# Pair attention layer on one core: front stage in two-part fp32r, separate semaphores for its loads, right values read back chunk by chunk, a seventh place for them in the mixing stage

## The reference

```
lk, rk, lv, rv = (x @ W_lk), (x @ W_rk), (x @ W_lv), (x @ W_rv)      # x: (2, 64, 64, 256), 8 heads of 32
scores = einsum('bxahd,bayhd->bxayh', lk, rk) / sqrt(32)
att    = softmax(scores, axis=2)                                      # over a
o      = einsum('bxayh,bxahd,bayhd->bxyhd', att, lv, rv)
...
```

## Time and profile before

| | |
|---|---|
| median of 3 runs | 3948.43 us (3945.7 to 3954.97) |
| the profiled execution: its own time | 3949.96 us |
| the profiled execution: span | 3947.9 us |
| PE busy | 3542.7 us (90%) |
| DVE busy | 2868.5 us (73%) |
| ACT busy | 2432.3 us (62%) |
| POOL busy | 1322.5 us (33%) |
| instructions fetched by DMA (q8) | 170 packets, 2.79 MB |
| DMA, 275 to 295 us, while batch 1's exponents are stored | 416 GB/s |

### The profile page before, as it was taken

How to read it: one execution, slowest core, us unless ns; L and a number is a source line. 1 busy time by engine, 2 the same in 40 slices (tenths; PEclk the granted TensorE clock), 3 DMA queues, 4 the chain that set the end, 5 groups by cost and what they waited for, 6 DMA issues and landing times. The chain is left out here.

```text
span 3947.9 us, 81665 instructions
## 1 busy us (share of the span) xinstructions
PE 3542.7 (90%) x30559; PEld 2953.9 (75%) x30559; DVE 2868.5 (73%) x4303; ACT 2432.3 (62%) x6245; POOL 1322.5 (33%) x740
## 2 busy tenths in 40 slices
PE   8986888788869988999999979999999979788887
PEld 5644555455549986888888868888888878788886
DVE  1457999899968874677777755777777766677787
ACT  3545888788855554666656655666666632677776
POOL 0007999899955552000000001000000014222254
PEclk9988999999989998999999989999999989899999
DMA  4583111311123333000000011000000046555565
GB/s 125 172 230 78 43 41 40 80 43 43 43 61 105 118 99 112 1 17 17 17 19 25 12 53 65 17 17 17 17 17 12 12 138 213 162 137 136 139 217 169
DMA packets 204756, 303.82 MB, mean 77 GB/s; under 512 B 18464, under 2 KB 156576, under 8 KB 201376
## 3 DMA queue, kind: packets, MB, share of 16 engines
q1 hardware_dynamic: 195232, 291.51, 24.7%
q10 hardware_dynamic: 9216, 8.39, 0.6%
HBM read 199.18 MB, written 100.66 MB: 76 GB/s over the span
## 5 line engine op out<-in xcount | busy, mean ns | idle before, releaser
L661 POOL TENSOR_TENSOR mx_big<-mp_lvs,mx_big 128x1280 f32<-128x1280 f32 (+1 forms) x256 | 802.0, 3205 | 335.0 <-ACT mp_lvs L587 317.1
L640 DVE TENSOR_TENSOR mx_big<-mp_psL,mx_big 128x2816 f32<-128x2816 f32 (+1 forms) x256 | 786.6, 3147 | 39.1 <-PE mp_psO L532 32.1
L594 ACT ACTIVATE mp_cut<-mp_psO,mx_mask 128x128 f32<-128x128 f32 x2048 | 551.0, 404 | 145.1 <-PE mp_psO L532 114.6
L532 PE MATMUL mp_psO<-mx_big,mp_pair 128*16 128x256 f32 x8192 | 501.5, 385 | 107.6 <-DVE mx_big L640 75.0
L1298 PE MATMUL sv_psO<-at_v_hi,sv_p_hi 128*128 128x258 f32 x2048 | 583.2, 285 | 13.2 <-DVE sv_p_lo L1386 10.1
L1298 PE MATMUL sv_psO<-at_v_lo,sv_p_hi 128*128 128x258 f32 x2048 | 578.1, 282 | 0.0
L1298 PE MATMUL sv_psO<-at_v_hi,sv_p_lo 128*128 128x258 f32 x2048 | 577.9, 282 | 0.0
L1317 ACT COPY sv_S<-sv_psS 128x512 f32<-128x512 f32 x512 | 300.5, 587 | 378.4 <-PE sv_psS L1272 260.7
L532 PEld LDWEIGHTS mp_psO<-mx_big,mp_pair 128*16 128x16 f32 x8192 | 330.1, 126 | 242.5 <-DVE mx_big L640 135.9
L1361 DVE TENSOR_TENSOR sv_run<-sv_run,sv_S 128x512 f32<-128x512 f32 x448 | 314.5, 702 | 248.1 <-ACT sv_S L1317 247.0
L1386 DVE TENSOR_TENSOR sv_p_lo<-sv_S,sv_p_hi 128x512 fp32r<-128x512 f32 x512 | 353.8, 691 | 108.4 <-ACT sv_p_hi L1326 107.4
(11 more groups left out here) (244 smaller groups left out, 7446.7 us busy)
## 6 DMA issues: line engine op xcount, KB each, us to landing
re_xg<-xg SPq DMA_DIRECT2D x192, 384.0 KB, 3.3
xg<-ga_xg SPq DMA_DIRECT2D x32, 768.0 KB, 4.0
att<-mx_big SPq DMA_DIRECT2D x16, 1024.0 KB, 5.5
mx_big<-rv SPq DMA_DIRECT2D x16, 1024.0 KB, 17.4
mp_pair<-att SPq DMA_DIRECT2D x128, 128.0 KB, 2.9
fr_xr<-in_x SPq DMA_DIRECT2D x16, 512.0 KB, 4.7
fr_xl<-in_x SPq DMA_DIRECT2D x32, 256.0 KB, 4.3
rv<-fr_rvs SPq DMA_DIRECT2D x16, 512.0 KB, 3.0
```

The lines of the kernel that those rows point to most:

```text
L532: mm = pe.matmul(psO[32 * j:32 * j + 2 * H, c % 2, q, :], pair[:, s, :, :, c * YC + y], Z[:, c % 2, y, :], start=True, stop=True, tile_pos ...
L594: ins = nc.scalar.activation(cut[:, s, c, :, h * DK:(h + 1) * DK], psO[:, c % 2, :, h * DK:(h + 1) * DK], ACT.Copy, scale=mask[:, h:h + 1])
L640: nc.vector.tensor_tensor(Z[:, c % 2, 0:m], psL[:, s, 0:D].unsqueeze(1).broadcast_to([P, m, D]), big[:, rv_slot(b, c), 0:m], ALU.mult).the ...
L661: nc.gpsimd.tensor_tensor(Z[:, c % 2, m:YC], lvs[:, s, :].unsqueeze(1).broadcast_to([P, YC - m, D]), big[:, rv_slot(b, c), m:YC], ALU.mult ...
```

## The change

- **fp32r parts.** The weights and the turned tiles of the front stage are kept as two fp32r parts, hi (a rounded copy, ACT) and lo (the value less hi, DVE), and each product is three fp32r matmuls (hi·hi, lo·hi, hi·lo) where it was one fp32 matmul. The original weights lie in `rvs`. PSUM `psT` is given free by DVE, after lo.
- **Order of a block.** PE: rk products, score of the block before, xl turned, rv products, xr of the *next* block turned, lk products. ACT: keep, xl hi, up to two exponents, two rvs copies, xr hi of the next block, the remaining exponents, two lk copies. DVE: two rk copies (now after the score of the block before), xl lo, the maximum, half of the block's subtractions and sums, xr lo of the next block, the other half.
- **Loads.** Own semaphores for ident and each weight; the xr tile of block 0 before the weights, xl after them; the three constants of the mixing stage last.
- **rv back.** Chunk 0 of batch 0 is read after block 14, chunk 1 when chunk 0 has landed, chunk 2 among the last stores, chunk 3 in the mixing stage behind pair 0's loads.
- **Late sums.** `PE_SUMS = (0, 8)`: all of batch 1's sum is on PE, 64 matmuls of 256 columns; DVE inverts straight from PSUM.
- **Mixing.** Seven places for rv (`seventh` is a buffer of its own). Chunks 0 to 2 of batch 1 are each loaded after two pairs' loads in the first pairs; chunk 3 at the change of batch, behind pair 33's x. Loads of x no longer wait for the memsets, which have the `pair` tiles ahead of `psO`. The loops of DVE and POOL start at pair 2.

```diff
+RV_SLOTS = 7
+Z_SLOT = 6
+def rv_place(big, seventh, b, c):
+
+    n = (b * (N // YC) + c) % RV_SLOTS
+    return seventh if n == RV_SLOTS - 1 else big[:, n]
...
-    PE_SUMS = (0, 5)
-    SUBS = {8: range(0, 6), 9: range(6, 13), 10: range(13, NHALF)}
-    EXPS = {9: range(0, 4), 10: range(4, 8), 11: range(8, 12), 12: range(12, NHALF)}
-    SUMS = {11: range(1, 8), 12: range(8, 12), 13: range(12, NHALF)}
+    PE_SUMS = (0, NC)
+    SUBS = {8: range(0, 4), 9: range(4, 9), 10: range(9, 14), 11: range(14, NHALF)}
+    EXPS = {9: range(0, 4), 10: range(4, 9), 11: range(9, 14), 12: range(14, NHALF)}
+    SUMS = {11: range(1, 4), 12: range(4, 9), 13: range(9, 14), 14: range(14, NHALF)}
...
+        w_hi = {n: fr.sb(f"w{n}_hi", [P, KT, D], F32R) for n in W}
+        w_lo = {n: fr.sb(f"w{n}_lo", [P, KT, D], F32R) for n in W}
+        xrT_hi, xrT_lo, xlT_hi, xlT_lo = (fr.sb(n, [P, KT, BLK], F32R) for n in ("xrT_hi", "xrT_lo", "xlT_hi", "xlT_lo"))
+        w = {n: rvs[:, i // 2, i % 2 * KT:(i % 2 + 1) * KT, :] for i, n in enumerate(W)}
...
-                sp.dma_start(*loads[0]).then_inc(w_in, 16)
-                load(0)
-                for dst, src in loads[1:]:
-                    sp.dma_start(dst, src).then_inc(w_in, 16)
-                load(1)
+                sp.dma_start(ident[:, :], ident_d).then_inc(ident_in, 16)
+                load_xr(0)
+                for n, src in (("rk", w_rk), ("rv", w_rv), ("lk", w_lk)):
+                    sp.dma_start(w[n][:, :, :], k_rows(src)).then_inc(w_in[n], 16)
+                load_xl(0)
+                load_xr(1)
+                load_xl(1)
+                for dst, src in mix_loads:
+                    sp.dma_start(dst, src).then_inc(mix_in, 16)
                 for j in range(NJ):
                     if j + 2 < NJ:
-                        load(j + 2)
+                        load_xr(j + 2)
+                        load_xl(j + 2)
...
-                        for c in range(N // YC):
-                            load_rv(sp, big, rv_d, 0, c, rv_back)
+                        load_rv(sp, big[:, 0], rv_d, 0, 0, rv_back)
+                sp.wait_ge(rv_back, 32)
+                load_rv(sp, big[:, 1], rv_d, 0, 1, rv_back)
                 for k in range(NC):
                     save(1, k)
-                sp.wait_ge(rv_back, 32 * (N // YC))
+                    if k == NC // 2 - 1:
+                        load_rv(sp, big[:, 2], rv_d, 0, 2, rv_back)
+                sp.wait_ge(mix_in, 16 * len(mix_loads))
+                sp.wait_ge(rv_back, 96)
...
+                def terms(hi, lo, xT_hi, xT_lo):
+
+                    return [(a, c, k) for k in range(KT) for a, c in ((hi, xT_hi), (lo, xT_hi), (hi, xT_lo))]
+
+                def units(g, n, xT_hi, xT_lo, done):
+                    for e, (a, c, k) in enumerate(terms(w_hi[n], w_lo[n], xT_hi, xT_lo)):
+                        mm = pe.matmul(psP[:, g, :], a[:, k, g * P:(g + 1) * P], c[:, k, :], start=(e == 0), stop=(e == 3 * KT - 1))
                     mm.then_inc(done, 1)
...
-                pe.wait_ge(w_in, 16 * len(loads))
+                def turn_xr(j):
+                    pe.wait_ge(xr_in[j % 2], (j // 2 + 1) * 16)
+                    reach(pe, xlT_kept, j)
+                    turn(xr, j % 2, xr_turned)
+
+                pe.wait_ge(ident_in, 16)
+                turn_xr(0)
                 for j in range(NJ):
-                    s = j % 2
-                    pe.wait_ge(xr_in[s], (j // 2 + 1) * 16)
-                    reach(pe, xlT_kept, j)
-                    turn(xr, s, xr_turned)
+                    pe.wait_ge(xrT_kept, j + 1)
+                    pe.wait_ge(w_cut, 1)
+                    for g in range(G):
+                        reach(pe, lk_kept, (j - 1) * G + g + 1)
+                        units(g, "rk", xrT_hi, xrT_lo, rk_made)
                     if j > 0:
                         score(j - 1)
-                    pe.wait_ge(xl_in[s], (j // 2 + 1) * 32)
-                    pe.wait_ge(xrT_kept, j + 1)
-                    turn(xl, s, xl_turned)
-                    for g in range(G):
-                        reach(pe, lk_kept, (j - 1) * G + g + 1)
-                        units(g, wrk, xrT, rk_made)
+                    pe.wait_ge(xl_in[j % 2], (j // 2 + 1) * 32)
+                    turn(xl, j % 2, xl_turned)
+                    pe.wait_ge(w_cut, 2)
                     for g in range(2):
                         pe.wait_ge(rk_kept, j * G + g + 1)
                         for t in range(2):
-                            for k in range(KT):
-                                mm = pe.matmul(psP[:, g, t * D:(t + 1) * D], xrT[:, k, (2 * g + t) * P:(2 * g + t + 1) * P], wrv[:, k, :],
-                                               start=(k == 0), stop=(k == KT - 1))
+                            rows = slice((2 * g + t) * P, (2 * g + t + 1) * P)
+                            for e, (a, c, k) in enumerate(terms(w_hi["rv"], w_lo["rv"], xrT_hi, xrT_lo)):
+                                mm = pe.matmul(psP[:, g, t * D:(t + 1) * D], c[:, k, rows], a[:, k, :], start=(e == 0), stop=(e == 3 * KT - 1))
                         mm.then_inc(rv_made, 1)
+                    if j + 1 < NJ:
+                        turn_xr(j + 1)
+                    pe.wait_ge(xlT_kept, j + 1)
+                    pe.wait_ge(w_cut, 3)
                     for g in range(G):
-                        if g == 0:
-                            pe.wait_ge(xlT_kept, j + 1)
                         pe.wait_ge(rv_kept, j * 2 + g + 1)
-                        units(g, wlk, xlT, lk_made)
+                        units(g, "lk", xlT_hi, xlT_lo, lk_made)
...
-                    for u in range(AB // 2):
-                        mm = pe.matmul(psS[:, 0, :], ident[:, :], E[1][:, r + 2 * u:r + 2 * u + 2, :].rearrange("p a f -> p (a f)"),
-                                       start=(k == 0 and u == 0), stop=(k == PE_SUMS[1] - 1 and u == AB // 2 - 1))
+                    for u in range(AB):
+                        mm = pe.matmul(psS[:, 0, 0:F], ident[:, :], E[1][:, r + u, :],
+                                       start=(k == 0 and u == 0), stop=(k == PE_SUMS[1] - 1 and u == AB - 1))
...
+                keep_xrT(0)
+                for n in ("rk", "rv", "lk"):
+                    act.wait_ge(w_in[n], 16)
+                    nc.scalar.copy(w_hi[n][:, :, :], w[n][:, :, :]).then_inc(w_hi_cut, 1)
                 for j in range(NJ):
-                    act.wait_ge(xr_turned, j + 1)
-                    nc.scalar.copy(xrT[:, :, :], psT[:, :, :]).then_inc(xrT_kept, 1)
+                    exps = list(EXPS.get(j, ()))
                     if j > 0:
                         keep(j - 1)
                     act.wait_ge(xl_turned, j + 1)
-                    nc.scalar.copy(xlT[:, :, :], psT[:, :, :]).then_inc(xlT_kept, 1)
-                    exps = list(EXPS.get(j, ()))
-                    for k in exps[:3]:
+                    nc.scalar.copy(xlT_hi[:, :, :], psT[:, :, :]).then_inc(xlT_hi_kept, 1)
+                    for k in exps[:2]:
...
+                    if j + 1 < NJ:
+                        keep_xrT(j + 1)
+                    for g in range(G):
                         if g == 0:
-                            for k in exps[3:]:
+                            for k in exps[2:]:
                                 exponent(0, k)
-                    for g in range(G):
...
                         dve.wait_ge(pe_summed, 1)
-                        for u in range(2):
-                            fold(den[:, b, 1 + u, :], last, psS[:, 0, u * F:(u + 1) * F])
-                            last = den[:, b, 1 + u, :]
+                        last = psS[:, 0, 0:F]
+                    else:
+                        dve.wait_ge(dve_summed, sums[0])
+                        fold(sum4[:, 0:2, :], sum4[:, 0:2, :], sum4[:, 2:4, :])
+                        fold(sum4[:, 0, :], sum4[:, 0, :], sum4[:, 1, :])
+                        last = sum4[:, 0, :]
...
+                keep_lo(0, xrT_hi, xrT_hi_kept, xrT_lo, xrT_kept)
+                for i, n in enumerate(("rk", "rv", "lk")):
+                    dve.wait_ge(w_hi_cut, i + 1)
+                    nc.vector.tensor_tensor(w_lo[n][:, :, :], w[n][:, :, :], w_hi[n][:, :, :], ALU.subtract).then_inc(w_cut, 1)
                 for j in range(NJ):
                     for g in range(G):
                         dve.wait_ge(rk_made, j * G + g + 1)
+                        if j > 0:
+                            dve.wait_ge(scored, j)
                         nc.vector.tensor_copy(rk[:, g, :], psP[:, g, :]).then_inc(rk_kept, 1)
-                        if j > 0:
-                            most(j - 1, g)
+                    keep_lo(j, xlT_hi, xlT_hi_kept, xlT_lo, xlT_kept)
+                    if j > 0:
+                        for u in range(2):
+                            most(j - 1, u)
                     if j == NC:
                         most_of_all(0)
-                    for k in SUBS.get(j, ()):
```

(51 more changed lines are left out.)

71 lines of the change are left out of this document (36 added, 35 removed).

## The result

The changed kernel takes **3913.12 us** (median of 4 runs, 3905.99 to 3916.29), the kernel before 3951.07 (4 runs): a ratio of 0.9902, 95% interval 0.9883 to 0.9922. The forecast was 3915, in a range of 3897 to 3936. The profiled execution is the fastest of its four, 3905.99 us with a span of 3904.2; the span fell by 43.7 us where the sum gave 34.8. So the median came within 2 us of the forecast, while the sum, which was made for the profiled execution, is 9 us off there.

The account below looks back on a forecast made before the run. PE was taken to bound the front stage, DVE to be nearly always busy in mixing. Front-stage blocks -38.4, gaps +8, lower level +7, tail +5.9, semaphores +0.3, mixing -2.2, -4.4, -11: 3949.96 - 34.8 = 3915 us, range 3897 to 3936.

Parts of the forecast that it names:

- Start: Front stage: PE starts its transposes at 5.5 us instead of 12.49, and rk at 10.7.
- Light blocks: Front stage, blocks 1 to 7: 12.35 us each instead of 13.74, PE waiting 0.6 us for DVE's xl lo.
- Heavy blocks: Front stage, blocks 8 to 14: DVE and ACT work makes them 103.5 us together, against 96.2.
- Gaps and lower level: Front stage: late instruction packets within scores cost +8 us (0 to 20), PE at its lower level afterwards +7 (0 to 10).
- some 3 of 15 blocks: Front-stage scores: about 26 of 128 positions of a packet's end make PE wait, 1 to 2 us each time.
- five such gaps: Heavy blocks: five idle gaps of PE ahead of rk, each followed by its lower level, +7 us together.
- The rival built on it: Front stage: instruction gaps and lower level don't come, so both +8 and +7 fall away: 3900 us, chance 0.20.
- Tail: End of front stage: with all late sums on PE, the inversion comes 5.9 us later after the first identity matmul.
- This cover is thin: End of front stage: third chunk and stores are done about 4 us before the norms, so cost nothing.
- Start of mixing: Mixing's start: PE released earlier, -2.2 us; pairs 0 and 1 wait less for x, -4.4 us (-5.9 to 0).
- Change of batch: Mixing: pair 33's x goes ahead of the only chunk left, removing PE's wait: -11 us (-11.2 to -8).
- Neither slower one: Front stage: PE at its lower level throughout (chance 0.03), or weight loads no longer hidden (0.01), each near 4050 us.

Follow-up runs that it names:

- Run 2: Changed kernel, but PE waits for all weights, the first xl tile and mixing's three constants before its first transpose: 3923.14 us.
- Run 1: Changed kernel with the front stage's products in plain fp32 again, the new order, loads and mixing kept: 3923.4 us.
- Run 6: Changed kernel with batch 0's maximum, exponential and sum jobs laid where DVE and ACT have nothing to do for PE: 3905.56 us.
- run 4: Changed kernel with 128 more instructions (32 small matmuls) on PE before its first transpose: 3943.0 us.
- 10: Changed kernel with batch 0's jobs in free places, batch 1's sums split between PE and DVE, and rv read back at blocks 13, 14 and 15: 3903.98 us.
- run 7: Changed kernel with chunk 2 of batch 1's values loaded at the change of batch with chunk 3, both ahead of pair 33's x: 3926.66 us.
- Run 3: Changed kernel with batch 1's late sums split again, five blocks on PE and three on DVE: 3911.8 us.
- run 8: Changed kernel with chunks 2 and 3 of batch 1's values both loaded at the change of batch, behind pair 33's x: 3915.78 us.
- run 12: Changed kernel with batch 0's jobs in free places, batch 1's sums split, and the wait for the last four stores moved into mixing: 3900.32 us.
- run 11: Changed kernel with only batch 0's values read back earlier, chunk 0 at block 13, chunks 1 and 2 at block 14: 3916.95 us.
- 9: Changed kernel with batch 0's jobs in free places and batch 1's sums split between PE (five blocks) and DVE (three): 3907.52 us.

## Why the prediction was right, and where its terms were off

- **Start: as forecast.** First transposes 5.72 (5.5), rk(0) 10.71 (10.7). Run 2 shows that the whole shift goes through.
- **Light blocks: as forecast**, 12.3 (12.35), at the pitch of the earlier trace rows, with PE waiting for DVE's xl lo, for 0.17 us and not 0.6 by the trace. Run 1 gives fp32r its part of it, 1.6 us a block.
- **Heavy blocks: the order of work was read rightly.** From rk(8) to rk(15) they took 15.7, 13.7, 14.6, 19.2, 14.7, 16.3 and 13.8 us where 15.6, 14.2, 15.3, 15.3, 14.8, 14.8 and 13.5 stood. Block 11 is over by its gap of 3.62 and the slow turn behind it, block 13 by rk products that fell to the lower level (records of 0.63 us, a granted clock of 0.67 from 187.4 to 191.6). Run 6 shows the cause to be the one named: with the jobs elsewhere, no wait for xr lo.
- **Gaps and lower level: the term that was mis-sized.** I allowed 8 + 7 = 15; rk(15) came at 217.44 against 212.7 without either, and the last score lost 1.4 more: 6.1 in all. That is nearly the whole distance of the profiled execution (3906) from 3915. The step that failed is "some 3 of 15 blocks": of 24 boundaries up to the last score, one made a gap of 3.9 us and one of 1.0, and no other within a score made more than 0.6. And of "five such gaps" with a lower level behind them, two showed in this execution, behind the gap and in block 13. The prediction counted positions. What the traces show is the time at which the next packet is fetched: the gaps from 2.5 us up all stand where stores or values fill the queues, and reach 7.7 us in run 4 and 8.2 before. A full queue is not the only condition, though. The gaps of 2.3 and 2.0 us before, at 705 (47.77 us) and 2497 (120.17 us), stand at a DMA share of 0.38 and 0.37 since the boundary before, which lay 6.6 and 5.1 us before the end of the gap; what made these two was not tried. The Trainium skill, "Runtime: NRT & Kernel Launch", section "Instruction fetch mechanics", calls the crossing mostly hidden: so it was for all but two here, but runs 4 and 10 show that it is not where stores or values fill the queues. The rival built on it (3900, chance 0.20) was the nearest to what happened in the profiled run.
- **That the median lies at 3913 is partly luck.** The profiled execution is 7 us below it. No trace of the slower ones was kept, but run 7's shows with the same front stage what can differ: its first product is 4.6 us later than the changed kernel's, with rk groups at the lower level where that one had them at the higher. The size of "lower level" is a matter of the single execution, which the sum did not see.
- **Tail: +7.1 where +5.9 stood**, from first identity matmul to inversion (30.42 against 23.33). The slow first records cost 2.8 us and not 1.8 (a granted clock of 0.50 to 0.53 from 241.7 to 247 us; before, 0.50 until 277 and 0.97 from there), and 128 records at 0.216 with 1.8 on top make 29.4, not 29.2. 1.35 came back in the norms, whose two groups of PE took 0.63 and 1.17 us straight behind the sums, at a granted clock of 1.00, where they took 1.06 and 2.07 before. "This cover is thin" was right: transfers ended at about 274 us, norms at 276.9. Run 3 shows why undoing this part brings only 2.6 us: the stores take over.
- **Start of mixing, pairs 0 and 1: -1.8 and -5.2** where -1.9 (with the semaphores) and -4.4 stood.
- **Change of batch: -11.1** where -11 stood; run 8 shows that the place of x alone would not have done it; whether the smaller amount alone would was not run.
- **Rivals.** Neither slower one left a mark: light blocks stayed at 12.3 us, at a PEclk of 1.00 in every 10 us window from 20 to 120, and 128x256 rows with a load each kept 0.12 us.

The two terms behind the first product were 0.9 us too small together, and 1.0 us lost after mixing, where nothing was changed, cancels that. Up to it: gaps and level -8.9, tail +1.2, norms -1.35, rest +0.1, which is the 9 us that the first product came earlier than the sum had it.

**Open.** Why reading values back runs at 210 GB/s where stores of attention reach 428 was not tried; the reads move in packets of 16 KB that take 1.3 us each, the stores in packets of 8 KB that take 0.3. Nor was it tried to place PE's boundaries with a few more or fewer instructions so that they miss the transfers.

## What to carry to other kernels

A stage that ends in a barrier ends with the last of its engines' chains *and* with the last transfer that its queue waits for: before shortening a chain, look up when the DMA share falls to zero, and move the wait for what the next stage doesn't touch to where it is touched (run 12). Work laid beside full DMA queues also delays the instructions of an engine that runs many short ones, so a load moved "into a free stretch" can cost more there than it saves at its old place (run 11). Edits that gained 12 and 7.6 us in their own stretch (runs 6 and 9) gave 3 and 1.5 us at its end until the bound behind them was moved. And before a few us between two single executions are put down to an edit, look for a stretch that the edit left alone and that differs too.
